# A message-passing layer with an indirect scatter: first units prepared apart, copies of x behind the weights, rows of x addressed by byte

## The reference

```python
rhat = edge_vec / (jnp.linalg.norm(edge_vec, axis=-1, keepdims=True) + 1e-12)
Y1 = SQ3 * rhat
emb = _radial_embedding(edge_length)          # 8 Gaussians, 0 beyond length 1
h = jax.nn.silu(emb @ mlp_w0 + mlp_b0)
h = jax.nn.silu(h @ mlp_w1 + mlp_b1)
w = (h @ mlp_w2 + mlp_b2).reshape(-1, 4, MUL)
ss, vv = xs[senders], xv[senders]             # x through W_up0, W_up1
m0 = w[:, 0] * ss
m1 = w[:, 1][:, :, None] * ss[:, :, None] * Y1[:, None, :]
m2 = w[:, 2][:, :, None] * vv
m3 = w[:, 3] * (jnp.einsum('emc,ec->em', vv, Y1) / SQ3)
msg_s = jax.ops.segment_sum(concat(m0, m3), receivers, num_segments=num_nodes)
msg_v = jax.ops.segment_sum(concat(m1, m2), receivers, num_segments=num_nodes)
out = concat(msg_s @ W_out0, msg_v @ W_out1) / 8 / AVG
x = _layernorm(x + out, axis=-1)
```

## Time and profile before

| | us |
|---|---|
| median of 3 runs | 1265.41 |
| lowest and highest | 1263.23, 1265.73 |
| the profiled execution: its time | 1268.42 |
| its span, first to last instruction | 1266.7 |

### The profile page before, as it was taken

The page is one execution under the profiler, slowest core; times in us unless marked ns, Lnnn a source line. Parts: engine busy times, 40 slices in busy tenths (PEclk is TensorE's granted clock), DMA queues, the critical chain, the costliest instruction groups (busy, mean ns, idle before and its releaser), DMA issues.

```text
span 1266.7 us, 31319 instructions
## 1 busy us (share of the span) xinstructions
PE 968.7 (76%) x6210; PEld 893.6 (71%) x6210; DVE 698.5 (55%) x2916; ACT 540.2 (43%) x1416; POOL 995.5 (79%) x792
## 2 busy tenths in 40 slices
PE   1888888787778887788777777888777868888880
PEld 1787777777777776677677676777676767778770
DVE  6764344466465565556555656646546556555532
ACT  4433223244435434525535534534443543553532
POOL 5378887878888888878888888888888888788885
PEclk9988788888877878878888978779878897777785
DMA  6466674434544444543453454444444454453444
GB/s 204 142 183 181 172 196 78 71 72 97 124 71 98 98 98 71 123 99 70 100 123 73 95 124 70 98 99 82 105 105 74 96 122 72 87 134 43 69 68 89
DMA packets 84975, 132.19 MB, mean 104 GB/s; under 512 B 17308, under 2 KB 69935, under 8 KB 84133
## 3 DMA queue, kind: packets, MB, share of 16 engines
q0 software_dynamic: 68304, 50.25, 29.9%
q1 hardware_dynamic: 14506, 78.09, 17.1%
q10 hardware_dynamic: 1963, 1.71, 0.5%
HBM read 78.35 MB, written 77.24 MB: 123 GB/s over the span
## 4 chain that ended last, share of the span: by engine, by line
POOL 42%; issue 26%; DMA 16%; SPq 10%; POOLq 5%; DVE 0%; ACT 0%
POOL acc L603 28%; DMA acc<-msg,index 14%; POOL sender L573 14%; SPq L380 6%; POOLq L579 3%; SPq L376 2%; SPq L404 2%; DMA acc<-in_x_dram 1%; POOLq L601 1%; POOLq L584 1%; POOLq L602 0%; SPq L426 0%; DMA total<-acc 0%; POOLq L88 0%; SPq L412 0%
## 5 line engine op out<-in xcount | busy, mean ns | idle before, releaser
L603 POOL DMA_INDIRECT acc<-msg,index x391 | 623.5, 1595 | 131.1 <-issue 106.9
L573 POOL DMA_INDIRECT sender<-in_x_dram,index x375 | 368.3, 982 | 128.3 <-issue 102.9
L730 PEld LDWEIGHTS ps_sum<-same,mid 128*128 128x128 f32 x1568 | 255.1, 239 | 10.0 <-DVE mid L1164 0.8
L730 PE MATMUL ps_sum<-same,mid 128*128 128x128 f32 x1568 | 260.2, 321 | 0.7 <-DVE mid L1164 0.7
L1149 DVE TENSOR_TENSOR wts<-ps_wts,bias 128x512 f32<-128x512 f32 x98 | 67.8, 692 | 283.5 <-PE ps_wts L717 283.5
L742 PE MATMUL ps_msg<-outw,sumT 128*128 128x64 f32 x1568 | 220.4, 302 | 0.0
L742 PEld LDWEIGHTS ps_msg<-outw,sumT 128*128 128x128 f32 x1568 | 216.1, 221 | 0.0
L1142 DVE TENSOR_TENSOR proj<-ps_up,vec_all 128x384 f32<-128x384 f32 x98 | 54.4, 555 | 223.5 <-PE ps_up L710 187.9
L827 ACT COPY sumT<-ps_sum 128x512 f32<-128x512 f32 x196 | 115.0, 587 | 146.4 <-PE ps_sum L730 143.7
L689 PE MATMUL ps_sT<-ident,sender 128*128 128x128 f32 x376 | 86.8, 307 | 115.1 <-DMA sender<-in_x_dram,index 114.3
L837 ACT COPY msg<-ps_msg 128x128 f32<-128x128 f32 x98 | 26.1, 266 | 336.1 <-DMA acc<-msg,index 243.1
(11 more groups left out here) (144 smaller groups left out, 1084.6 us busy)
## 6 DMA issues: line engine op xcount, KB each, us to landing
acc<-in_x_dram SPq DMA_DIRECT2D x40, 625.0 KB, 4.8
total<-acc SPq DMA_DIRECT2D x30, 832.0 KB, 4.8
out_dram<-normed SPq DMA_DIRECT2D x29, 832.0 KB
by_row<-in_x_dram SPq DMA_DIRECT2D x1408, 0.5 KB
by_row<-in_x_dram ACTq DMA_DIRECT2D x640, 0.5 KB
acc<-msg,index POOLq DMA_INDIRECT x391, 3.4
sender<-in_x_dram,index POOLq DMA_INDIRECT x375, 6.0
out_dram<-normed ACTq DMA_DIRECT2D x1, 832.0 KB
```

Of the source, the lines that this page charges most:

```text
L573: pool.indirect_dma_start(sender[:, u % SRING, i, :], None, x, bass.IndirectOffsetOnAxis(ap=index[:, u, 0, i:i + 1], axis=0)).then_inc(fet ...
L603: pool.indirect_dma_start(acc, bass.IndirectOffsetOnAxis(ap=index[:, v, 1, i:i + 1], axis=0), msg[:, v % RING, i, :], None, compute_op=ALU.add
L730: mm = pe.matmul(ps_sum[r][:, i, h, :], mid[:, b, 2 * r + i, P * h:P * (h + 1)], same[:, b, 2 * r + i, :], start=True, stop=True)
```

## The change

On POOL four units (`EARLY = 4`) are gathered before the first scatter and two units (4 and 5) after the scatters of unit 0. On PE unit 1 has an order of its own, in which `sums` and `project_out` of unit 0 come before `project_up`, `hidden1` and `radial` of unit 1. On ACT unit 0 is staged as soon as the basis of the first 32 tiles (eight units) is there; the basis of the other 360 tiles is computed in units 2, 3 and 4. On DVE the table is made in two parts, `compare_tiles` inside unit 0 and the rest behind unit 0's products; clipping and directions of the later tiles come behind units 1 and 3, and `make_dense_orders` behind unit 3. On SP the weights come before `zeros` and the first two copies, eight of the weight loads go to ACT's queue, and the third and later copies wait until unit 1's senders' rows are transposed. Row numbers for the single rows in the loops are multiplied by 512 once (`scale_ids`), so that a DMA's address is the loaded value; the rows of the first two such units stay as they were.

The diff, cut to its core:

```diff
+EARLY = 4
+NARROW = 8
+ROW_BYTES = D * 4
+        FIRST_TILES = NARROW * G
+        def rows_at(engine, kind, u, i, starts, a, n):
+            _, starts = nc.values_load_multi_w_load_instructions(starts[:, a:a + n], ...)
+            for p in range(n):
+                engine.dma_start(by_row[a + p:a + p + 1, row_slot(u, i), :].bitcast(U8),
+                                 x_bytes[bass.ds(starts[p], ROW_BYTES)].rearrange("(a d) -> a d", a=1)
+                                 ).then_inc(row_in[row_slot(u, i)], 16)
 # SP
-            sp.wait_ge(zeroed, 1)
-            sp.dma_start(acc[N:N + SPARE, :]..., zeros[:, :, :]).then_inc(spare_rows, 16)
-            for k in range(PIECES_FIRST):
-                copy(k // 2, k % 2, waits=k >= 2)
             sp.wait_ge(consts, 1)
...
+            sp.wait_ge(zeroed, 1)
+            sp.dma_start(acc[N:N + SPARE, :]..., zeros[:, :, :]).then_inc(spare_rows, 16)
+            for k in range(PIECES_FIRST):
+                copy(k // 2, k % 2, waits=k >= 2)
             sp.wait_ge(src_in, 16)
+            sp.wait_ge(senderT_ps, 2)
+            sp.sem_inc(sp_passed, 1)
             for h in range(PIECES_FIRST // 2, PIECES // 2):
...
-                if h == 2 + P // SP_ROWS:
+                if h == 1:
                     load_ids()
 # POOL
-            for u in range(AHEAD):
+            for u in range(EARLY):
...
-                for u in range(v + AHEAD, min(v + AHEAD + ROW, UNITS)):
+                for u in range(v + AHEAD if v else EARLY, min(v + AHEAD + ROW, UNITS)):
 # PE
+            def first_message(u, k):
+                hidden0(u, k)
+                sums(u - 1, k - 1, 0)
+                sums(u - 1, k - 1, 1)
+                pe.wait_ge(weights, 6)
+                project_out(u - 1, k - 1)
+                project_up(u, k)
+                hidden1(u, k)
+                radial(u, k)
+                turn(u + 1, k + 1)
 # ACT
+            act.wait_ge(consts, 1)
+            for h in range(2):
+                (the eight loads of mlp1, mlp2, bias0, bias1)
...
             for u in range(IN_LOOP):
                 unit(u, u)
+                if u == 2:
+                    act.wait_ge(dve_pre, LATER_CLIP)
+                    squares(later, range(NB // 2))
+                if u == 3:
+                    squares(later, range(NB // 2, NB)).then_inc(act_pre, 1)
+                if u == 4:
+                    act.wait_ge(act_pre, 4)
+                    act.activation(basis_all[:, later, :], ..., ACT.Exp, scale=-0.5).then_inc(act_pre, 1)
 # DVE
+            def scale_ids():
+                dve.wait_ge(ids_in, 16 * len(ID_LISTS))
+                for ids, units, i, apart in ID_LISTS:
+                    dve.tensor_scalar(ids, ids, float(ROW_BYTES), None, ALU.mult).then_inc(ids_scaled, 1)
...
-            directions()
+            directions(first, 5, 1)
             equal_receivers(0, 0)
-            unit(0, 0)
+            unit(0, 0, following=False)
+            make_scatter_orders()
+            equal_receivers(1, 1)
             unit(1, 1)
+            clip(later, 7)
+            unit(2, 2)
+            unit(3, 3)
+            directions(later, 10, 2)
+            scale_ids()
             make_dense_orders()
-            with dve.Fori(1, PAIRS - 1) as j:
+            with dve.Fori(2, PAIRS - 1) as j:
```

More of the change, by code:

```diff
@@ L794, in _, with squares, scale_out @@
                 mm.then_inc(act_planes, 1)
+            def squares(tiles, of):
+                for k in of:
+                    mm = act.activation(basis_all[:, tiles, k], len_clip[:, tiles], ACT.Square, scale=float(NB - 1),
+                                        bias=minus_k[:, k:k + 1])
+                return mm
+            first, later = slice(0, FIRST_TILES), slice(FIRST_TILES, TILES)
             act.wait_ge(dve_pre, 3)
[L797 to L800 removed]
+            squares(first, range(NB)).then_inc(act_pre, 1)
             act.wait_ge(act_pre, 1)
[L802 to L815 removed]
+            act.activation(basis_all[:, first, :], basis_all[:, first, :], ACT.Exp, scale=-0.5).then_inc(act_pre, 1)
+            def scale_out():
+                act.wait_ge(loaded, 16 * WEIGHT_DMAS)
+                by = 1.0 / (AVG * (2 * MUL) ** 0.5)
+                for k in range(4):
+                    for h in range(2):
+                        rows = slice(MUL * k, MUL * (k + 1))
+                        y = 3 ** 0.5 if k == 2 or (k == 0 and h == 1) else 1.0
+                        mm = act.mul(outw[rows, h, :], out_raw[rows, h, :], by * y)
+                    mm.then_inc(weights, 1)
             def stage(u, k):
@@ L857, in unit @@
                 b = k % 2
+                if k == 0:
+                    act.wait_ge(loaded, 16 * WEIGHT_DMAS)
                 if not tail:
@@ L921, in pair @@
                     unit(2 * j + part, k + part, meanwhile=dense, body=body)
+            act.wait_ge(prepared, 1)
+            act.wait_ge(act_pre, 2)
             stage(0, 0)
             stage(1, 1)
+            act.wait_ge(loaded_up, 16 * UP_DMAS)
+            act.mul(mlp0[:, :, :], mlp0_raw[:, :, :], NB ** 0.5).then_inc(weights, 1)
+            act.mul(up[:, :], up_raw[:, :], MUL ** -0.5).then_inc(weights, 1)
+            act.wait_ge(dve_pre, 5)
+            act.activation(norm[:, :], norm[:, :], ACT.Sqrt).then_inc(act_pre, 1)
             turned(0, 0)
@@ L982, in _, with clip @@
             mm.then_inc(prepared, 1)
+            dve.tensor_copy(dump_rowf[:, :], dump_row[:, :]).then_inc(dump_ready, 1)
+            def clip(tiles, before):
+                dve.tensor_scalar(len_clip[:, tiles], len_all[:, tiles], 0.0, 1.0, ALU.max, ALU.min).then_inc(dve_pre, 1)
+                dve.tensor_scalar(beyond[:, tiles], len_all[:, tiles], 1.0, FAR, ALU.is_gt, ALU.mult).then_inc(dve_pre, 1)
+                dve.wait_ge(dve_pre, before + 2)
+                dve.tensor_tensor(len_clip[:, tiles], len_clip[:, tiles], beyond[:, tiles], ALU.add).then_inc(dve_pre, 1)
+            first, later = slice(0, FIRST_TILES), slice(FIRST_TILES, TILES)
+            dve.wait_ge(act_planes, 1)
+            clip(first, 0)
+            dve.wait_ge(prepared, 1)
+            dve.wait_ge(dump_ready, 1)
+            dve.tensor_tensor(gap_all[:, :, :], wide(dump_rowf[:, :], 1, UNITS), dst_all[:, :, :], ALU.subtract
+                              ).then_inc(prepared, 1)
+            dve.wait_ge(act_planes, 4)
+            dve.tensor_tensor(vec_sq[:, :, :], vec_all[:, :, :], vec_all[:, :, :], ALU.mult).then_inc(dve_pre, 1)
+            dve.wait_ge(dve_pre, 4)
+            dve.tensor_reduce(norm[:, :], vec_sq[:, :, :], AX_X, ALU.add).then_inc(dve_pre, 1)
             dve.wait_ge(ends_ps, 2)
@@ L1147, in products @@
                 receiver_rows(u, k, 1)
+                if k == 0:
+                    compare_tiles()
+                    dve.wait_ge(loaded, 16 * WEIGHT_DMAS)
                 dve.wait_ge(wts_ps, u + 1)
```

148 lines of the change are left out of this document (72 added, 76 removed).

## The result

| | before | after |
|---|---|---|
| median of 6 runs, us | 1265.49 (1263.23 to 1266.62) | 1258.74 (1257.46 to 1259.99) |
| ratio, 95% interval | | 0.9947 [0.9937, 0.9957] |
| profiled execution, us (span) | 1268.42 (1266.7) | 1257.46 (1255.7) |
| first scatter | 54.10 | 39.90 |
| first scatter of unit 1 | 69.35 | 57.64 |

The change takes 6.75 us off, 0.5%. The forecast was a gain of 10.8 (1254.7 us). The time lies inside the range, 4 us above the forecast.

What follows compares the result with a forecast made beforehand. POOL was taken as the bound from 80 us to the last scatter. First scatter 16.3 us sooner, less 5.0 for gathers, less 0.5, gives 10.8; 1257.6 profiled, 1254.7 against the median of runs, range 1250.5 to 1260.5.

Steps and rivals of the forecast that it cites:

- Start: POOL's first scatter moves from 54.1 to 37.8 us, 16.3 sooner, with table and message 0 arriving within a microsecond.
- The mark on PE: PE's first L696 (now L714) of unit 0 starts at 21.4 us against 35.66, 14.3 us sooner.
- the signs that I named: First scatter near 37.8, unit 1's 20.3 later, then 0.3 us gaps; PE mark near 21.4; table and message within 1.5.
- The clock of PE: PE reaches its higher clock about 10 us after unit 0's start; at the lower, first scatter 39.5 at worst.
- Four gathers, 5.0: Four gathers that were free now stand after unit 0's scatters on POOL and cost 5.0 us.
- I keep it: POOL's 2.68 us landing wait before the fourth scatter stays, beside two copies; without the collision, a gain of 2.4.
- 0.5 for DVE's later work: DVE's multiply for 360 later tiles lengthens one or two POOL instructions: 0 to 1.5 us, taken as 0.5.
- Byte offsets: Single rows by byte offset drop a register computation per row on SP and ACT; priced at nothing.
- The copies' new place: The third and later of 40 copies come some 11 us later on SP; priced at nothing.
- Message 4: Rival: message 4, put at 90 against POOL at 94.9, comes late; 1258 to 1260; 0.22 together with a later start.
- The earlier start: Rival: edges land two microseconds sooner, first scatter 1.5 sooner; also without the 2.68 wait 1250.5 to 1253; chance 0.12.
- slower than before: Rival: layer norm's loads late on SP, DVE stalls and messages with it; 1268 with 13 us felt; chance 0.06.

Runs made afterwards that it cites:

- again: The changed kernel as it is, run once more with a second profile: 1258.74 us, ratio to before 0.9948, first scatter 37.87.
- wide: The changed kernel with basis, clips and directions of all tiles first, as before the change: 1267.66 us, ratio to before 1.0022, first scatter 49.53.
- early5: The changed kernel with EARLY = 5, five units of rows gathered ahead of the first scatter instead of four: 1251.44 us, ratio to before 0.9891.
- held: The changed kernel, SyncE's pair of copies of 57.54 held until unit 1's first scatter has landed: 1255.63 us, ratio to before 0.9931.
- raw_rows: The changed kernel with row numbers instead of byte offsets in the loops, DVE's multiply left out: 1258.81 us, ratio to before 0.9945.
- before_bytes: The kernel before with the byte offsets of the rows alone: 1267.78 us, ratio to before 1.0015.
- copies_first: The changed kernel with SyncE's clearing and first pair ahead of the weights, second pair without its wait, as before: 1258.76 us, ratio to before 0.9949.
- early5_held: The changed kernel with EARLY = 5, third and fourth pairs of copies held for the landings of tiles 0 and 4: 1251.46 us, ratio 0.9896.

## Why the prediction held, and where it failed

**Start: right.** The mark on PE (L714 of unit 0) was put at 21.4 and came at 22.25 and, in again, 21.37. The squares and Exp were put at 1.65 and 0.5 and took 1.85 and 0.42. `mid` of unit 0 was put at 31.2 and ended at 31.82 and 31.00; the table at 36.3: 36.55. The first scatter was put at 37.8, and came at 37.87 and 39.90. For the lower clock I wrote 39.5 at worst; my own terms give 40.5 (37.1 and 3.4 more), as 39.5 would be the message's end, which came at 38.94. That 37.87 lies so near 37.8 is in part luck: the table ended 0.6 us sooner than I put it in again (35.74), and POOL took 2.13 us from there, where I had 1.5. wide shows that the narrow basis is two thirds of it. Of the signs that I named, a first scatter near 37.8 and the mark on PE came true. Table and message ended 0.1 us apart in again, but 2.4 in the first profile; unit 1 came 17.7 and 19.1 us behind unit 0 and not 20.3; and the gaps were not of 0.3 us only.

**The clock of PE: half right.** I wrote that PE would have reached its higher clock by the sums, 10 us after unit 0's start. In again it had: the eight matmuls of L735 at 26.40 took 1.13 us, the sums 2.05. In the first profile it had not: L735 at 27.28 took 2.04, and the sums, 10.1 us after the mark, 3.78. What decides it isn't shown by these runs.

**Four gathers, 5.0: right in size.** Eight gathers fill 47.53 to 57.64, so four take 5.05. But I counted them as a given cost of the change, and early5 shows that they need not have been one: POOL's 10.44 us of idle time ahead of the first scatter could hide them.

**"I keep it": the term that failed.** I saw that copies would be issued beside unit 0's scatters and kept the wait of 2.68 us as it was. I treated it as one wait at one place. It is a wait for either of units 0 and 1, and its length hangs on the distance to a pair within 1 or 2 us, and on how many scatters stand between issue and need: two in unit 0, one in unit 1. In the changed kernel the two waits were 0.41 and 3.47 in one profile and 1.59 and 5.50 in the other, against 2.68 and 0.74 before. That is 0.5 and 3.7 us more than I kept. For again the sum then closes: 16.23 sooner, less 5.05, less 3.67 is 7.5, and unit 2 is 7.74 us sooner; the medians say 6.75. For the first profile: 14.20 less 5.05 less 0.46 is 8.7, and unit 2 is 9.12 sooner. So the 4 us that I forecast too much have no single source: in again the start was as forecast and the waits took 3.7 us; in the first profile the start itself was 2.1 us short of the forecast, by PE's lower clock and the later edges, and the waits took 0.5. held gives back 2 to 3 us, but it isn't the measure of this term: its two waits (0.53 and 0.52) lie 2.4 us below the 3.42 that I kept.

**"0.5 for DVE's later work": right in size, but covered.** The later multiply ran from 63.37 to 64.65, while POOL waited for a landing anyway, so nothing of it could be felt. In early5 POOL did not wait: the gather at 61.75, beside the multiply (60.97 to 62.25) and the first rescaling (62.28 to 63.03), took 1.40 us, where the one before it took 0.98 and the next 0.94. Which of the two instructions made it longer isn't shown. The Trainium skill's page "SBUF — State Buffer", section "Who interferes with whom", says that a tensor_scalar can lock GpSimd out for its whole length. In the first profile the rescaling of the row numbers did not: it ran at 64.69 and 65.43, and the scatter at 64.72 took 1.55 and the gather at 66.58 1.01 us, as elsewhere; raw_rows, without it, has the same time.

**Parts priced at nothing.** Byte offsets: right in the changed kernel (0.07 us). "Even with the saving gone nothing would be lost" looked only at POOL's waits from 80 us on; before_bytes lost 1.9 us, has a new wait at 72, and the cause of its loss is open. The copies' new place: right (copies_first), as far as their start goes. That they came later was weighed only by who waits for their data, and not by what they run beside.

**Rivals.** Message 4 was put at 90 and ended at 89.30, `mid` of unit 4 at 80.0 (79.44); POOL came for it at 97.08, so the rival didn't happen. `mid` of unit 3, which I put at 58.5, ended at 58.86, but the terms that I named for it (31.2, three times 7.5, table 5.1, clipping 1.3) already sum to 60.1, so that this step was right by luck. The Trainium skill's page "ScalarE: Activation LUTs", section "What ACT_TABLE_LOAD costs", would have the two switches cost 5.3 us; the rows show loads of 1.28 each at 69.31 and 73.22, hidden behind DVE's planning, and no drain beside them that reached a message. The earlier start didn't come either: the edges were cast at 12.03 in the first profile, 0.96 later than before, and at 11.07 in again, as before, though copies no longer travel beside them. Layer norm: first load put at 219 (218.19), reader at 236 (237.79), slower than before did not happen.

**Profile against medians.** I subtracted the 3.0 us by which the profiled execution of before lay above its median. The result needed that: 1268.4 less 11.0 is the profile of after, but the medians differ by 6.75. (1257.6 less 3.0 is 1254.6; the forecast says 1254.7.)

## What to carry to other kernels

Where an engine bound by a steady stream also waits for landings near the start, list all large transfers with their dates beside all its waits, for the kernel before and for the dates that you forecast: an edit that shifts either by a microsecond or two moves the collision to another place and gives back some of the gain, and holding the bulk transfer a few microseconds can win it back (2 to 3 us in held; nothing that could be told in early5_held, whose waits were short already). Count also what stands between an issue and the instruction that needs its landing: where it is least, a late landing is felt first. When a start is moved forward, fill the idle time that is left ahead of it before counting work moved behind it as its price. And one profile of a start isn't enough: two of one kernel differed by 2 us in the first scatter.

## What the runs showed of the hardware

A scatter-add of one tile, whose median landing was 3.4 us, was awaited for up to 9 us (56.98 to 66.09 in again) when it was issued within a microsecond of two DRAM-to-DRAM copies of 625 KB; with the copies held it took at most 4.1. Within 0.4 us of a pair unit 1 waits longer than unit 0 (3.47 to 5.50 us against 1.30 to 2.68), but most of that is the kernel's order, not the transfer: with one scatter less between issue and need POOL comes for the landing 1.9 us sooner. From issue to the end of the wait it was 7.1 to 9.1 us in unit 1 and 6.7 to 8.1 in unit 0. Why it is still 1.7 to 2.1 us longer in unit 1 within one profile (9.11 against 7.02 in again, 8.38 against 6.73 in raw_rows) stays open. The instruction's own time on POOL hardly changed, 1.62 to 1.72 us: the delay is seen only in who waits for the landing.

The granted clock of PE stands as 1.00 from 20 to 30 us in the first profile of after, where the eight matmuls of L728 took 2.08 us against 1.11 at 37.88. The row of that window (busy us of PE, PEld, DVE, ACT and POOL with instructions, then PE's clock):

```profile
20.00:30.00 10.00, 8.71 (x35) 7.10 (x34) 8.10 (x31) 6.73 (x19) 6.59 (x7) 1.00 0.18 44
```

In again the same column says 0.71 for these 10 us, though the eight matmuls took 2.08 us there too. So near the start the durations of like rows tell PE's level, and the column doesn't.
